# A gated running state added on GpSimd, with the row statistics taken one step later

## The reference

```python
def _L0_attn_ref(x, W_qkv, b_qkv, W_gate, b_gate):
    qkv = jnp.einsum('bsd,ed->bse', x, W_qkv) + b_qkv
    q, k, v = jnp.split(qkv, 3, axis=-1)
    kv_state = jnp.cumsum(k * v, axis=1)
    g = jax.nn.sigmoid(jnp.einsum('bsd,ed->bse', x, W_gate) + b_gate)
    return q * kv_state * g

x = x + _L0_xattn_ref(_layernorm(x), ctx_1024, ctx_1024, ...)
x = x + _L0_attn_ref(_layernorm(x), ...)
x = x + _L0_ffn_ref(_layernorm(x), ...)
```

## Time and profile before

| | |
|---|---|
| median of 3 runs | 486.77 us (486.44 to 487.39) |
| span of the profiled execution | 485.6 us |
| median less span | 1.2 us |
| VectorE busy | 446.5 us, 92% of the span |
| TensorE busy | 383.7 us, 79% |
| ScalarE busy | 361.3 us, 74% |
| GpSimd busy | 8.1 us, 2%, 25 instructions |

### The profile page before, as it was taken

The page is one execution under the profiler, slowest core; times in us unless marked ns, Lnnn a source line. Parts: engine busy times, 40 slices in busy tenths (PEclk is TensorE's granted clock), DMA queues, the critical chain, the costliest instruction groups (busy, mean ns, idle before and its releaser), DMA issues.

```text
span 485.6 us, 5951 instructions
## 1 busy us (share of the span) xinstructions
PE 383.7 (79%) x1877; PEld 303.2 (62%) x1880; DVE 446.5 (92%) x686; ACT 361.3 (74%) x950; POOL 8.1 (2%) x25
## 2 busy tenths in 40 slices
PE   0796757998997997997997997991999789637754
PEld 0585546886885886885886885891986445313333
DVE  4559999999999999999999999999998869899993
ACT  1359887998998988988978888885437577666764
POOL 2100100000000000000000000000000000000000
PEclk9999887999999999999999999996799999868888
DMA  7930500040140040040041041022020000000001
GB/s 234 355 103 1 173 0 2 24 129 23 34 135 7 22 130 22 12 137 26 5 132 39 2 130 45 1 90 85 0 88 0 0 3 0 1 0 0 24 22 43
DMA packets 27070, 27.65 MB, mean 57 GB/s; under 512 B 1184, under 2 KB 26784, under 8 KB 27040
## 3 DMA queue, kind: packets, MB, share of 16 engines
q1 hardware_dynamic: 26736, 27.27, 17.7%
q0 software_dynamic: 160, 0.01, 0.0%
q10 hardware_dynamic: 144, 0.00, 0.0%
HBM read 26.22 MB, written 1.05 MB: 56 GB/s over the span
## 4 chain that ended last, share of the span: by engine, by line
DVE 75%; issue 11%; PE 8%; ACT 5%; POOL 1%; POOLq 0%
DVE focus_words L1247 8%; DVE focus_words L1263 8%; DVE sorted L1286 4%; DVE level L1272 4%; DVE level L1273 4%; DVE merge L1299 4%; DVE sorted L1287 4%; DVE sorted L1191 3%; DVE amax L1160 2%; DVE sorted L1292 2%; DVE sorted L1291 2%; DVE keymax L1289 2%; DVE merge L1297 2%; PE bank L808 2%; DVE rank L1310 2%
## 5 line engine op out<-in xcount | busy, mean ns | idle before, releaser
L808 PE MATMUL bank<-WkT,rows_T 128*128 128x256 f32 x512 | 127.1, 396 | 32.9 <-ACT rows_T L426 32.9
L808 PEld LDWEIGHTS bank<-WkT,rows_T 128*128 128x128 f32 x512 | 96.8, 197 | 50.4 <-ACT rows_T L426 38.5
L902 PE MATMUL bank<-ctx_words,focus_words 128*128 128x257 f32 x512 | 115.6, 384 | 3.5 <-ACT focus_words L525 3.5
L902 PEld LDWEIGHTS bank<-ctx_words,focus_words 128*128 128x128 f32 x512 | 99.7, 197 | 16.2 <-ACT focus_words L525 5.5
L513 ACT ACTIVATE focus_words<-focus_words,shift,ff 128x256 f32<-128x256 f32 x136 | 79.8, 590 | 0.6
L479 ACT ACTIVATE focus_words<-bank 128x256 f32<-128x256 f32 x136 | 50.2, 381 | 27.3 <-PE bank L808 27.3
L525 ACT ACTIVATE focus_words<-focus_words,row_scale 128x256 f32<-128x256 f32 x136 | 56.2, 513 | 12.8 <-DVE row_scale L1265 12.8
L426 ACT ACTIVATE rows_T<-bank 128x512 f32<-128x512 f32 x78 | 44.4, 595 | 18.4 <-PE bank L781 18.4
L1247 DVE SCALAR_TENSOR_TENSOR focus_words<-focus_words,key_and,key_xor 128x2048 int32<-128x2048 int32 x17 | 39.9, 2345 | 8.2 <-ACT focus_words L479 8.2
L781 PE MATMUL bank<-ident,ctx_words 128*128 128x128 f32 x256 | 38.4, 279 | 3.8 <-DMA ctx_words<-in_ctx_dram 3.1
L1330 DVE TENSOR_TENSOR mask<-focus_words,fifth 128x2048 bf16<-128x2048 f32 x17 | 39.0, 2292 | 0.5
(11 more groups left out here) (192 smaller groups left out, 586.3 us busy)
## 6 DMA issues: line engine op xcount, KB each, us to landing
ctx_words<-in_ctx_dram SPq DMA_DIRECT2D x32, 512.0 KB, 3.9
ctx_words<-in_L_ffn_gate_w_dram SPq DMA_DIRECT2D x2, 1024.0 KB, 7.9
ctx_words<-in_L_ffn_up_w_dram SPq DMA_DIRECT2D x2, 1024.0 KB, 8.8
xs<-in_x_dram SPq DMA_DIRECT2D x4, 256.0 KB, 5.0
ctx_words<-in_L_ffn_down_w_dram SPq DMA_DIRECT2D x2, 512.0 KB, 9.5
ctx_words<-in_L_ffn_down_w_dram SPq DMA_DIRECT2D x1, 1024.0 KB, 5.0
out_dram<-xs SPq DMA_DIRECT2D x3, 256.0 KB, 2.1
gateT<-in_L_attn_W_qkv_dram SPq DMA_DIRECT2D x1, 512.0 KB, 6.3
```

The source lines that it names most:

```text
L808: ins = pe.matmul(proj_bank[m][:, t * D:(t + 1) * D], rows_T[:, m % 2, 2 * t + k, :], WT[:, k, :], start=(k == 0), stop=(k == KT - 1))
L902: ins = pe.matmul(sum_bank[k][:, 0:GW], heads_half(expo[slot][:, t, :], k), ctx_ring[:, s, t, :], start=(s == 0 and t == 0), stop=(s == PE ...
```

## The change

GpSimd gets a loop over the eight tiles that adds `gated_sum` into `xs`, each add waiting for the product of its tile (`gated_ready`, new) and for the attention add of its batch (`attn_added`), and counting up `running_added`. On VectorE `add_running(t)` is left with the product, which no longer waits for itself; for t of 2 and more it first waits until the add of tile t - 2 has read the buffer. The statistics become a function of their own, `running_stats(t)`, that waits for the add, and the written-out order puts them behind another piece of work where there is one: tile 0 behind `scale_weight(2)`, 1 behind `gate_tile(3)`, 2 behind `weight_codes(2)`, 4 behind `gate_tile(6)`, 5 behind the four-bit codes of the lower half, 6 behind the product of tile 7. Those of tiles 3 and 7 follow at once. TensorE's wait for the bank asks for the product in place of the add.

```diff
--- before.py
+++ after.py
@@ -259,6 +259,7 @@
         gate_read = sem("gate_read")
         kv_prod_ready = sem("kv_prod_ready")
         running_in_psum = sem("running_in_psum")
+        gated_ready = sem("gated_ready")
         running_added = sem("running_added")
         x_fp4_ready = sem("x_fp4_ready")
         gate_in_psum = sem("gate_in_psum")
@@ -411,6 +412,10 @@
 
             pool.wait_ge(expo_ready, CGROUPS + 1)
             pool.memset(x_hat2[:, :, D - 1:D], 1.0).then_inc(ones_in_last, 1)
+            for t in range(T):
+                pool.wait_ge(gated_ready, t + 1)
+                pool.wait_ge(attn_added, t // 2 + 1)
+                pool.tensor_tensor(xs[:, t, :], xs[:, t, :], gated_sum[:, t % 2, :], ALU.add).then_inc(running_added, 1)
 
         @block.scalar
         def _(act):
@@ -970,7 +975,7 @@
                 if t == 1:
                     pe.wait_ge(attn_added, PAIRS)
                 if t >= 2:
-                    pe.wait_ge(running_added, t - 1)
+                    pe.wait_ge(gated_ready, t - 1)
                 dst = oct_bank[t % 2][:, 0:D]
                 if t % 2:
                     pe.matmul(dst, ones[:, :], kv_prod[:, t - 1, :], start=True, stop=False)
@@ -1421,8 +1426,10 @@
             def add_running(t):
                 dve.wait_ge(running_in_psum, t + 1)
                 dve.wait_ge(gate_read, t + 1)
-                then(dve.tensor_tensor(gated_sum[:, t % 2, :], oct_bank[t % 2][:, 0:D], q_gated[:, t, :], ALU.mult))
-                dve.tensor_tensor(xs[:, t, :], xs[:, t, :], gated_sum[:, t % 2, :], ALU.add).then_inc(running_added, 1)
+                if t >= 2:
+                    dve.wait_ge(running_added, t - 1)
+                dve.tensor_tensor(gated_sum[:, t % 2, :], oct_bank[t % 2][:, 0:D], q_gated[:, t, :], ALU.mult)\
+                    .then_inc(gated_ready, 1)
 
             def hidden(i):
 
@@ -1439,8 +1446,7 @@
                 dve.tensor_tensor(q_gated[:, t, :], bank[2 + 2 * (t % 2)][:, 0:D], sig[:, t, :], ALU.mult)\
                     .then_inc(gate_read, 1)
 
-            def run(t):
-                add_running(t)
+            def running_stats(t):
                 dve.wait_ge(running_added, t + 1)
                 row_stats((t,))
 
@@ -1529,18 +1535,22 @@
             mix(3)
             gate_tile(1)
             weight_codes(1)
-            run(0)
+            add_running(0)
             scale_weight(2)
+            running_stats(0)
             add_batch(3)
             mean_variance(2)
             refine_for_act(2)
             gate_tile(2)
-            run(1)
+            add_running(1)
             gate_tile(3)
-            run(2)
+            running_stats(1)
+            add_running(2)
             weight_codes(2)
+            running_stats(2)
             gate_tile(4)
-            run(3)
+            add_running(3)
+            running_stats(3)
             mean_variance(3)
             refine(3)
             normalise_rows(LOWER)
@@ -1548,17 +1558,21 @@
             settle()
             row_block_scales(0)
             scale_to_fp4(half_rows[0], blk_rcp[:, half_blocks[0]], lower)
-            run(4)
+            add_running(4)
             gate_tile(6)
-            run(5)
+            running_stats(4)
+            add_running(5)
             cut_to_code(3, lower)
             settle()
             clip_q(lower)
             settle()
             times_fp8(3, x_fp4, x_fp4_ready, lower)
+            running_stats(5)
             gate_tile(7)
-            run(6)
-            run(7)
+            add_running(6)
+            add_running(7)
+            running_stats(6)
+            running_stats(7)
             mean_variance(4)
             refine(4)
             normalise_rows(UPPER)
```

## The result

The kernel after takes 482.87 us, median of 4 runs (482.2 to 483.63), beside 487.08 us (486.44 to 488.35, 4 runs) of the kernel before: a ratio of 0.9904, interval 0.9889 to 0.9918. That is 4.2 us faster by the medians and 4.7 by the ratio, where 1.0 us slower was forecast. The span of the profiled execution is 480.4 us, its own time 482.2, the shortest of the four. In every execution for which both are on record 1.7 to 1.9 us lie between span and time, not the 1.2 taken ahead of the prediction; the profiled execution of the kernel before, with a span of 485.6, was thus a long one of its kind, and the two spans differ by 5.2 us, more than the medians do.

A forecast was written before the change was run, and what follows sets the result against it. VectorE, 75% of the chain, was taken to bound the kernel, its tail a relay with ScalarE. Terms 0.26 (tile 0), 0.71 (tile 3) and 0.07 (tile 7) summed to +1.04 us: 487.8 us, range 486.3 to 489.2.

The forecast's parts named there:

- One hidden cost: GpSimd loads code: Tail: the add may need a 9.1 us code load, ending at 367.2, 15 us ahead of need, so hidden.
- a rival: Alternatives: port free 487.0 us (chance 0.25), slow add 489.1 (0.07), quick add 486.2 (0.07), code load exposed 494.8 (0.03).
- The price of an add: One 128x256 add on GpSimd: 0.70 us duration, plus 0.10 handover in and 0.05 out.
- c: Time from the end of VectorE's product to the earliest start of statistics: 0.85 us, between 0.45 and 1.30.
- Tile 0: Tail's start: GpSimd's add waits until VectorE's third-weight scaling ends, delaying statistics and attention add: a loss of 0.26 us.
- held up: Tile 0's add cannot run beside VectorE's two-SBUF-input scaling; the main case, 487.8 us, chance 0.55.
- Tiles 1 and 2: Tile 1: nothing gained or lost; tile 2's statistics move from idle time onto the chain behind the weight codes, +0.35 us.
- Tile 3: Nothing stands between its product and statistics, so VectorE waits for the add: statistics 0.71 us later.
- Tiles 4 and 5: VectorE's waits for ScalarE absorb add 4 and a clipping held up to 0.7 us by add 5: zero.
- the cover: VectorE's wait for ScalarE ahead of tile 7's gate product, 0.86 us before; without it a 0.7 us loss.
- Tiles 6 and 7: Tile 7's product waits for TensorE's sum; tile 6's statistics fit that wait; tile 7's statistics 0.07 us later.
- VectorE's handed-over work: Eight adds, 3.7 us of VectorE work, mostly off the chain; at tiles 3 and 7 it returns as waits.

The follow-up runs named there:

- the three runs: Kernel after plus an all-reduce at its end, 489.22 us; kernel before plus an iota at its end, 481.85; kernel before with its all-reduce replaced by an add, 481.34.
- after_5: The kernel after, unchanged, measured again on one chip beside the kernel before (487.52 us): 482.39 us, ratio 0.9901.
- scale_first: Kernel after with scale_weight(2) ahead of tile 0's product and tile 0's statistics behind the attention add: 481.22 us, ratio 0.9870 to the kernel before.
- stats_moved_only: Kernel after's order with the adds back on VectorE and a 16-column iota at GpSimd's end: 481.74 us, ratio 0.9887 to the kernel before.

## Why the prediction was wrong, step by step

**The step that failed is "One hidden cost: GpSimd loads code".** It read the 9.1 us behind the memsets as the price of a load, and asked where in the tail such a load would fall. Two questions were not asked. Who waits for the load that is already there? The prediction read the waits of the tail alone; those of the first 30 us say that TensorE waited 15.2 us for GpSimd. And why does a load stand at the start at all, when something must have been in place? Because, by the theory that the three runs bear out, the last execution had left the other set. The term that is missing from the sum is -5.93; with it the forecast's +1.04 becomes -4.9, and the spans differ by -5.2 (the medians by -4.2; after_5 beside its own kernel before by -5.1). Neither did a rival cover it, so the range held no time below 486.3.

What the forecast says of the load in the tail is borne out. The configuration came at 337 us, right behind the last memset, and not, as worked out, behind the first attention add; both lie far ahead of 376.4. In the runs 6.2 to 7.7 us passed from the instruction before to the first call of the other set when that call waited for nothing else, 9.1 and 10.6 at the start, and nothing was left to pay where 40 us lay between configuration and call. The Trainium skill (GPSIMD Engine Reference, Instruction dispatch) says that the first call of freshly loaded code pays about 6 us; the trace agrees at the low end of what was seen inside the kernel (6.2 us) and not at its start (9.1), and the last case shows that the load need not wait for the call.

**The price of an add** was right: 0.72 us for 0.70, 0.08 in and 0.04 out, c = 0.84 for 0.85 (product ends at 395.04, statistics start at 395.88). The duration was luck in part: it was a choice between 0.56 and 0.84, taken in the middle. (The price of two gate products, given there from the earlier trace rows, stands in the earlier trace rows.)

**Tile 0: right, held up.** The first add ended 0.57 us behind the scaling, not 0.70, perhaps since part of it was already done while it was held: a loss of 0.14 for 0.26. Beside VectorE's scaling, two inputs in SBUF, the add took 2.68 us; beside the attention add of scale_first, with one, it took 0.73. That is the Trainium skill's rule (SBUF — State Buffer, Who interferes with whom), and the trace agrees. One input in SBUF isn't always free, though: see add 5 below.

**Tiles 1 and 2: right.** The codes of the third weight wait 1.20 us for ScalarE's step, where it was 0.60.

**Tile 3: right.** +0.66 for +0.71.

**Tiles 4 and 5: right in sum.** The bf16 clipping, one tensor in and out of SBUF, takes 0.83 us beside add 5, which itself takes 0.84 and not 0.72; without an add on GpSimd it takes 0.43 in the same order (stats_moved_only). The forecast had it start late, it is drawn out instead. The wait ahead of gate tile 7 shrinks from 0.86 to 0.71, so the cover held.

**Tiles 6 and 7: right.** Product of tile 7 waits for TensorE, statistics +0.08 for +0.07.

**VectorE's handed-over work** (3.3 us less busy, 446.5 to 443.2) bought nothing, as said: it turned into waits, 1.9 us of them for GpSimd.

## What to carry to other kernels

Before costing a change of GpSimd's program, list which of its instructions change the loaded code, who waits at the start of the kernel for GpSimd, and which set is in place at the end: as these kernels were timed, the end of GpSimd's program decided how the next start went, and a 16-column iota at the end was worth 6 us. What an execution behind another program takes was not tried; by the theory it would hang on the set that the other program leaves. And a handed-over instruction is worth only what its engine is not then made to wait: put independent work of VectorE behind it, but nothing long with two operands in SBUF.

## What the runs showed of the hardware

- How long GpSimd's first select waits goes with the set that the program's last instruction needed. In the kernels that end with the select's set, or have only one, it follows the configuration instruction within 0.1 us; in the two that end with the other set, after 8.9 and 10.3 us. Later in the kernel a change of set took 6 to 8 us. That the code stays in place from one execution to the next is inferred from this.
- A VectorE instruction with two inputs in SBUF that started first holds up a GpSimd instruction that reads SBUF to its end: 2.22 us for an add of three columns, 2.68 for one of 256 that takes 0.72 alone. Beside a bf16 VectorE instruction with one input both were drawn out, 0.83 for 0.43 us and 0.84 for 0.72.
- The end of this kernel takes 66.6 to 67.3 us where the mean granted TensorE clock of the last 10 us is 0.82 or 0.83, and 68.0 to 68.5 where it is 0.66. Between the two lie about 1.2 us, more than the change costs in the tail (0.88).
